# Loading an output projection matrix in its own row order, and reordering its columns on TensorE

## The reference

```
h = tok(log_dt, x, B, inv_A_real, A_imag)              # 64 x 128 x 1024, a sum over 64 modes
h = h + attn(layernorm(h), wq, wk, wv, wo)             # 32 query heads and 8 key/value heads of 32
h = h + ffn(layernorm(h), W_base, b_base, lora_A, ...) # 1024 x 1024 and four routed low-rank parts

def attn(x, wq, wk, wv, wo):
    q, k, v = x @ wq.T, x @ wk.T, x @ wv.T ; q, k = rope(q), rope(k)
    out = softmax(mask(q @ k.T / sqrt(32))) @ v        # per head; a head's 32 columns lie together
    return out.reshape(b, s, 1024) @ wo.T              # wo is 1024 x 1024
```

## Time and profile before

| | us |
|---|---|
| median of 3 runs | 2982.34 (2980.67 to 2982.85) |
| the profiled execution's own time | 2979.9 |
| its span, first to last instruction | 2978.1 |
| mean granted TensorE clock | 0.983 of full speed |

### The profile page before, as it was taken

How to read it: one execution, slowest core, us unless ns; L and a number is a source line. 1 busy time by engine, 2 the same in 40 slices (tenths; PEclk the granted TensorE clock), 3 DMA queues, 4 the chain that set the end, 5 groups by cost and what they waited for, 6 DMA issues and landing times.

```text
span 2978.1 us, 62015 instructions
## 1 busy us (share of the span) xinstructions
PE 2830.5 (95%) x16986; PEld 1404.8 (47%) x16986; DVE 2465.3 (83%) x8697; ACT 1893.8 (64%) x5933; POOL 1969.6 (66%) x1734
## 2 busy tenths in 40 slices
PE   4777899999999999999999999999999999999987
PEld 3665444444444444444444444444444444444433
DVE  8998788888888888888888888888888888888873
ACT  5885666666666666666666666666666666666652
POOL 3441477777766777767777667776777776777763
PEclk9998899999999999999999999999999999999999
DMA  7976477766666666666666666666666666666662
GB/s 194 226 200 164 97 147 152 147 147 147 144 154 148 142 151 146 148 150 145 149 147 145 152 148 143 150 147 150 147 148 148 148 145 152 147 145 148 142 135 64
DMA packets 1254304, 442.92 MB, mean 149 GB/s; under 512 B 1200961, under 2 KB 1210049, under 8 KB 1254097
## 3 DMA queue, kind: packets, MB, share of 16 engines
q1 hardware_dynamic: 1254096, 441.02, 66.0%
HBM read 88.55 MB, written 67.11 MB: 52 GB/s over the span
## 4 chain that ended last, share of the span: by engine, by line
PE 47%; DVE 19%; issue 12%; POOL 9%; ACT 7%; DMA 3%; SPq 1%; DVEq 0%; ACTq 0%; POOLq 0%
PE bank_b L1673 23%; PE bank_a L1673 14%; ACT probs L1249 5%; DVE heads L1455 5%; DVE probs L1401 4%; PE bank_c L1673 4%; POOL p_hl L1162 3%; POOL probs L1158 3%; PE score L1640 2%; DMA tok_h<-kout 2%; PE pv L1662 2%; DVE share L1410 2%; POOL rope_a L1168 2%; PE kps L490 1%; POOL xy_hl L1177 1%
## 5 line engine op out<-in xcount | busy, mean ns | idle before, releaser
L1249 ACT ACTIVATE probs<-probs,negmax 128x128 f32<-128x128 f32 x2048 | 789.8, 387 | 261.7 <-DVE negmax L1401 261.7
L1162 POOL TENSOR_TENSOR p_hl<-probs,p_hl 128x512 f16<-128x512 f32 x512 | 615.7, 1202 | 344.7 <-ACT p_hl L1258 342.5
L1158 POOL TENSOR_TENSOR probs<-probs,rsum 128x512 f32<-128x512 f32 x512 | 556.5, 1087 | 219.1 <-DVE rsum L1412 218.0
L1673 PE MATMUL bank_a<-qkv_hi,xt 128*128 128x512 f16 x2048 | 653.6, 381 | 1.8 <-DMA xt<-xy_hl 1.8
L1401 DVE CUSTOM_DVE_ANT_0 probs<-score,table,scal 128x128 f32<-128x128 f32 x2048 | 596.4, 348 | 43.9 <-issue 43.1
L1673 PE MATMUL bank_b<-b_hi,yt 128*128 128x512 f16 x2016 | 630.7, 379 | 0.0
L1258 ACT ACTIVATE p_hl<-probs 128x512 f16<-128x512 f32 x512 | 319.9, 625 | 420.6 <-POOL probs L1158 409.3
L1455 DVE TENSOR_TENSOR heads<-rope_a,heads 128x512 f16<-128x512 f32 x320 | 398.8, 1262 | 28.1 <-ACT heads L1279 28.1
L1673 PE MATMUL bank_b<-o_hi,at_hi 128*128 128x512 f16 x1024 | 389.1, 380 | 1.5 <-ACT at_hi L1264 1.5
L1673 PE MATMUL bank_a<-qkv_lo,xt 128*128 128x512 f16 x1024 | 389.5, 380 | 0.0
L1673 PE MATMUL bank_b<-o_lo,at_hi 128*128 128x512 f16 x1024 | 389.1, 380 | 0.0
(11 more groups left out here) (210 smaller groups left out, 4518.0 us busy)
## 6 DMA issues: line engine op xcount, KB each, us to landing
tok_h<-kout SPq DMA_DIRECT2D x64, 512.0 KB, 6.1
hin<-tok_h SPq DMA_DIRECT2D x64, 512.0 KB, 3.2
r<-tok_h SPq DMA_DIRECT2D x64, 512.0 KB, 3.7
out_dram<-r SPq DMA_DIRECT2D x63, 512.0 KB, 3.0
probs_t<-p_hl SPq DMA_TRANSPOSE x512, 3.1
xc<-in_x_dram SPq DMA_DIRECT2D x32, 128.0 KB, 4.2
raw_a<-in_L_attn_wq_dram SPq DMA_DIRECT2D x1, 4096.0 KB, 13.8
raw_b<-in_L_attn_wo_dram SPq DMA_DIRECT2D x32, 128.0 KB, 3.7
```

The source lines that it names most:

```text
L1158: TT(x, x, rsum[:, u % 4].unsqueeze(2).to_broadcast([P, GR, T]), ALU.mult).then_inc(s_norm, 1)
L1162: TT(p_hl[:, u % 2, 1], probs[:, u % 4], p_hl[:, u % 2, 0], ALU.subtract).then_inc(s_plo, 1)
L1249: ins = A(probs[:, u % 4, g], probs[:, u % 4, g], ACT.Exp, bias=negmax[:, u % 4, g:g + 1], scale=-1.0, accum_out=sums[:, u % 4, g:g + 1])
L1673: ins = MM(bank, x(c), w[:, c, cols], start=(c == 0 and i == 0), stop=(c == KC - 1 and i == 2))
```

## The change

`load_wo` now takes one block of `wo`, 128 whole rows, and puts it into `raw_b` as it lies: 128 runs of 4 KB. There are eight such loads, one in each of chunks 0 to 7. The heads then lie in their original order, so a job for `wo` can't turn 128 adjacent columns any more. In its place PE makes 16 products of 32 columns each with the identity matrix. The 32 columns are the stationary operand, the identity the moving one, and `tile_position` puts the result on PSUM partitions 32k to 32k+31, that is, into one of four column groups of the array. The result in the bank is the one that the four transposes gave; nothing changes for ACT and DVE. The waits for `wo_in` count 8 loads in place of 32.

```diff
-        def load_wo(h):
-            to = h // 16 * 512 + h % GR * P + h // GR % 4 * HD
-            sp.dma_start(raw_b[:, :, to:to + HD],
-                         w["wo"].rearrange("(i p) k -> p i k", p=P)[:, :, h * HD:(h + 1) * HD]).then_inc(w["wo_in"], 16)
+        def load_wo(i):
+            sp.dma_start(raw_b[:, i], w["wo"][i * P:(i + 1) * P]).then_inc(w["wo_in"], 16)
...
             if exists(ch):
-                for h in range(3 * ch, min(3 * ch + 3, HQ)):
-                    load_wo(h)
+                if ch < NO:
+                    load_wo(ch)
...
-                dve.wait_ge(w["wo_in"], 16 * HQ)
+                dve.wait_ge(w["wo_in"], 16 * NO)
...
-                for c in range(4):
-                    ins = nc.tensor.transpose(place(j)[:, c], raw[:, (4 * a + c) * P:(4 * a + c + 1) * P], idt)
+                if name == "o":
+
+                    for c in range(GR):
+                        for k in range(4):
+                            at = (16 * a + GR * k + c) * HD
+                            ins = nc.tensor.matmul(place(j)[32 * k:32 * k + 32, c], raw[:, at:at + HD], idt,
+                                                   start=True, stop=True, tile_position=(0, 32 * k))
+                else:
+                    for c in range(4):
+                        ins = nc.tensor.transpose(place(j)[:, c], raw[:, (4 * a + c) * P:(4 * a + c + 1) * P], idt)
```

More of the change, by code:

```diff
@@ L809, in turn @@
                 if i == 0 and a == 0 and j < J_B:
-                    pe.wait_ge(w["qkv_in"] if j == 0 else w["wo_in"], 48 if j == 0 else 16 * HQ)
+                    pe.wait_ge(w["qkv_in"] if j == 0 else w["wo_in"], 48 if j == 0 else 16 * NO)
                 if j >= J_B:
```

## The result

| | us |
|---|---|
| before, median of 20 runs | 2982.52 |
| changed, median of 20 runs | 2987.05 (2981.69 to 2990.03) |
| ratio, with its 95% interval | 1.0015 [1.0009, 1.0022] |
| profiled execution of the changed kernel, its span | 2983.7, 2981.9 |

The interval lies above 1, so the kernel is slower, by 2.7 to 6.6 us. The forecast was +6.8 us. But a job did not take the 1.76 us on which that sum stood. It took half of it, and the loss came from places that the sum didn't have.

The account below looks back on a forecast made before the run. PE fills the main loop, unchanged; DVE paces the token stage, and PE, ACT, DVE and maxima through memory the weight stage. Terms -2.35 + 9.2 = +6.8 us gave 2986.7 for the profiled execution, 2989 for the median, 8-in-10 range 2979 to 3022.

Parts of the forecast that it names:

- The price of a product: PE's jobs for `wo`: products overlap two at a time, 1.76 us a job, 3.5 us at 1.2 GHz; chance 0.45.
- PE starts its products in order: Jobs for `wo`: a product's second record waits for its first; only the next product's first runs beside it, two at a time.
- the lower bound of the forecast's own range: Jobs for `wo`: all four column groups at once, 0.88 us a job.
- rival 2: Jobs for `wo`: all four column groups work at once, 0.88 us a job; 0 to +4.4 us, say 2984.5; chance 0.20.
- The rule of the Trainium skill: Column groups: tiles load weights and multiply in parallel, up to 4x for 32 columns; by it 0.88 us a job.
- First place: Jobs 24 to 31, begun at 1.2 GHz: costlier products make PE end +10.0 us later and DVE +9.3, hidden by nothing.
- Second place: Jobs 32 to 39: three fill PE's wait for `o_lo` at no cost; the other five take 8.8 us.
- `ps_ar` at full clock: `ps_ar` after job 39: 32 records in 5.0 us at 2.4 GHz, 7.4 before, as PE works nearly without a gap.
- The 2.1 us that the forecast let come back: First to second score group: the stretch is about 2.1 us shorter at full clock.
- Token stage: Relieved queues let the store behind DVE's first stall, before 150.32, land in time: -2.35 us; second stall left.
- SP falling behind: Token stage: SP's chunk takes 12.10 us, 0.45 more than DVE's 11.65, until DVE has to wait.
- its own test: Jobs for `wo`: forecast wrong if a job's time is not between 1.6 and 2.2 us, or the main loop's time changes.

Follow-up runs that it names:

- exchanged loops: Changed kernel with a job's two loops exchanged, so eight records for one column group stand in a row; 1.0047 against the kernel before, +14 us.
- second trace: The changed kernel itself, unaltered, timed and traced once more beside other kernels; 1.0014 against the kernel before, +4.2 us.
- 128 columns: Changed kernel with four f32 products of 128 columns a job, 8 records in place of 32, column reordering left out; 0.9998 against the kernel before.
- the loads alone: Kernel before with the eight loads of 4 KB runs, its four transposes a job kept, column reordering left out; 0.9996, -1.2 us.
- 32 issues with long runs: Kernel before with 32 loads, each 32 whole rows in 4 KB runs, transposes kept, column reordering left out; 0.9994, -1.8 us.
- the four kinds of loads: Loads of `wo` with transposes kept, against before: 32 short runs 0, 32 long -1.8, 8 short +4.8, 8 long -1.2 us.

## Why the number was right and the reason wrong

**The price of a product: wrong.** The number was right by luck. The step that failed is "the first of product k+1, in the next group, can run beside it, and its second waits again", from "PE starts its products in order". Measured: 0.86 us a job, the lower bound of the forecast's own range and rival 2's value. Rival 2's range, 0 to +4.4 us at a chance of 0.20, ends 0.1 us below the measured +4.5, though it had no stop either. The rule of the Trainium skill that stands in the forecast, its page "TensorEngine Tiling (Array Packing)", held for f32 too, with 32 records in the time of 8. The exchanged loops are the only order in which something near the forecast's time was seen, 1.87 us, and by another mechanism.

**First place: +9.3 forecast, +3.6 for DVE and +4.2 for PE measured.** The first three jobs ran at 1.2 GHz and took 1.7 us each; the other five 0.97 us each, and the clock rose within the fourth. The stretch at 1.2 GHz was longer than before in this trace, 5.8 us to 4.2. In the changed kernel's second trace it was 4.6 us, and its eight jobs took 9.35 us and not 9.96. In the other traces with these products the place cost 8.6 to 9.5 us, with transposes 5.8. In the runs, with transposes in jobs 32 to 39, none of this is seen (-1.5 us).

**Second place.** The first three jobs filled a wait, as forecast (the wait is 4.05 us, 5.68 before). The other five and the stop took 299.17 - 290.76 = 8.41 us, 4.69 before: +3.7 us. The forecast said 8.8, from 1.76 us a job. The true parts are about 6.3 us of products, partly at 1.2 GHz, as with 128 columns (6.11), and 2.1 us of stop, for which the sum had no term.

**`ps_ar` at full clock: wrong.** The forecast's reason was that PE works nearly without a gap; there was the wait of 4.05 us and then the stop. It took 6.94 us, not 5.0, with the clock at 0.51 from 301.6 on. With 128 columns, without a stop, it took 6.0 and the clock fell at 301.1, so the stop is not its only cause. The 2.1 us that the forecast let come back failed with it: from the first to the second score group it is 8.47 us, 7.85 before.

**Token stage: not shown.** In the first pair of traces it is -2.5 us against -2.35, and the stall near 150 us went, with the queue below 85%. But the same kernel's second trace starts its jobs for `wo` at 260.76, where the kernel before did at 260.81, and in the runs the loads alone give -1.2 us, with zero in the interval. That the first pair met the forecast's -2.35 is chance. And the forecast's picture of SP falling behind is not borne out: 32 issues with long runs leave DVE the fewest waits of the four kinds of loads, 1.4 us, in one trace of each.

**The sum.** The forecast's terms were -2.35 + 9.2. In the first pair of traces they are -2.5 at the first job, +4.2 for PE in the first place, -0.2 from there to job 35, +3.7 from job 35 to `ps_ar`, -0.5 in `ps_ar` and +0.6 behind it: +5.3 at the second score group. Too dear a product covered for a missing stop and a low clock. The forecast named its own test, a job between 1.6 and 2.2 us, and by that test it was wrong. It also read the clock's rise before as 264.30; it was 265.0, which alone would change little.

**What stays open.** What makes the stop, beyond its tie to 256 records, its place in the stream and the transfers that land with its piece. Why the kernels without a stop lose 3 us in their traces (the table's 51.4 to 52.0) and no more than 0.6 us in medians timed beside transposes, where single traces start their jobs up to 6 us apart. Why products in both places cost 4 us where those in either cost at most 1. And how much of the last 2 to 3 us of the changed kernel is clock and how much order.

## What to carry to other kernels

Small f32 products into the four column groups cost what one wide product costs, if neighbours in the program go to different groups; blocks of one group in a row cost twice that (1.87 us a job and 0.87). Many small instructions where few stood need a look at the instruction stream's own supply: count records, and search for an idle engine released by nothing. And a saving of 2 us in one stage, read from one pair of traces, may not be there in the next: trace the same kernel twice before building a sum on it.

## What the runs showed of the chip that was not expected

- By the assignment of records to groups above, PE starts a product for a free column group ahead of about three queued for a busy one (1.87 us a job with the loops exchanged, 3.5 if strictly in turn, 0.87 if free).
- A 16 KB piece of the instruction queue took 0.94 to 0.97 us at four places of the changed kernel, one of them with the data queue 64.8% busy, and 2.95 us at 294.9, with the data queue all but idle (0.3%); in other kernels it took up to 5.6 us there. A stored row of maxima came back at the same moment, 7.9 us after it was issued. Why is open; DMA transposes had been issued some microseconds before.
- Of the same 4 MB, 128-byte runs kept the queue at 96 to 97% and 4 KB runs at 79 to 87%, with 32 issues as with 8 (65 to 160 us, the loads of `x` and the stores included).
- The clock was at 1.2 GHz in all fourteen kept traces when the jobs for `wo` began, wherever that was between 258.3 and 271.5 us, and rose 2.9 to 5.8 us later. With 128 columns it fell at 301.1 us inside `ps_ar`, though PE had been busy without a gap since 291.13.
- Beside a POOL copy of 1.03 us one DVE instruction took 0.76 us longer, in 12 chunks of 16, and not where the copy had ended before it.
